# Features of a second group of tokens computed earlier, and its first MLP ahead of its second softmax, in a transformer kernel on one core

## Chip, core and metric

One core of one Trainium2 chip runs the whole program in one launch. The metric is device time in microseconds, from three runs without a profiler; one further execution was recorded by the hardware profiler, and all rows below are from that one.

## What is computed

The input x has 8 sequences of 256 tokens with 256 features. It passes through four attention layers with an MLP each, then a cross attention and a composed MLP. The change touches the first layer alone. What a layer does, cut from the reference:

```python
x = x + self_attention(layer_norm(x, ln1_g[i], ln1_b[i]), Wq[i], Wk[i], Wv[i], Wo[i], bo[i])
h = layer_norm(x, ln2_g[i], ln2_b[i])
x = x + (jax.nn.gelu(h @ W1[i] + b1[i], approximate=False) @ W2[i] + b2[i])
```

Of the eight heads, four are local (softmax over the own and the previous block of 128 tokens, causal), four are linear: with q = softmax(q) over the 32 features of a head and k = elu(k) + 1, in buckets of 64 tokens,

```python
k_cum = jnp.cumsum(bk.sum(axis=-2), axis=-2)
ctx = jnp.cumsum(jnp.einsum('bhund,bhune->bhude', bk, bv), axis=2)
ctx = ctx / (k_cum[..., None] + 1e-06)          # then shifted by one bucket
out = jnp.einsum('bhund,bhude->bhune', bq, ctx)
```

## The kernel before

The 2048 tokens are four groups of 512 (two sequences, four tiles of 128 tokens). A step takes group n through attention while group n - 1 goes through the first matmuls of its MLP and group n - 2 through the second. Every product of 32-bit operands is made of three passes over a high and a low part (`PASSES`), so each matrix that feeds TensorE is split: ScalarE copies the high part, VectorE or GpSimd subtracts it to get the low part. There is no scheduler: each engine has its list of calls, written out by hand, and runs it in order; an engine that waits for a semaphore holds up all that is behind it. The first two steps have their own lists, `first_step` and `second_step`, on TensorE, ScalarE and VectorE; GpSimd uses the general `step`.

The parts, by name, for group n: `pe_qk` (L1427) makes the transposed queries and keys of the local heads; `pe_tok` (L1432) makes, tile by tile, values of all heads and queries and keys of the linear heads (512 columns), which `act_tok` copies into `v8` and `qk`. **Features**: `dve_features` (maximum of each query head, L644, and subtraction, L646), `act_features` (exponentials of keys and queries), `dve_features2` (relu of the keys L651, joining step min-and-add L653 which raises `kf_done`, sum L656, reciprocal, scaling L660 which raises `qn_done`). `pe_qnt` transposes the queries, `pe_ctx` makes the contexts, `dve_ctx` divides them, `pe_lin` applies them, and the result is split by `act_lin_hi` (L1131) and `dve_lin_lo` (L615). **Softmax** of the local heads, for each sequence b of the group: `pe_s` (scores, L1460), `dve_max` (two reductions, L686 and L687), `act_exp` (eight exponentials with sums, L1137), `pe_pt` (transposes, L1502), `act_pt` and `dve_pt` (copies of the transposed probabilities into `pt[b]`), `pe_pv` (products with the values, L1519). `act_pspread` and `pe_pnorm` turn the reciprocals of the sums. `pe_wo` is the output projection, `dve_res1` adds it to x, after GpSimd's `pool_bias`. **Norms**: `ln_moments`, then rstd on GpSimd (`pool_rstd`, L446), then `ln_centred` (L602) and `ln_shifted` (L611); index 0 is the norm ahead of attention (vec_a), 1 that of the MLP (vec_f). **MLP**: `pe_xt` transposes, `pe_h` the eight first products, `act_gelu` a gelu and the high part, `pool_h_lo` the low part on GpSimd (L458). A gelu waits until the low part two before it is done, and `pe_h` of chunk m for the gelu of chunk m - 2. GpSimd's list around the MLP of group 0 is: rstd of its norm, two bias additions, rstd of group 2's first norm, four low parts, a bias addition, four low parts, the low parts of W2.

`pe_busy` (L1564) repeats a matmul of an identity matrix whose result nobody reads.

Much of SBUF is one array, `scratch`, cut into overlapping tiles. `pt[1]` covers columns 1056 to 2592, the same as `qk` (1056 to 2080) and `qexp` (2080 to 2592). The second of the tiles `xh`, columns 7712 to 8736, holds the normed tokens of the MLP's norm.

## Time and profile before

| what | us |
|---|---|
| median of three runs | 977.26 (976.57 to 978.7) |
| the profiled execution | 977.58 |
| its span, first to last instruction | 975.7 |
| TensorE busy | 953.2 (98%); first slice of 24 us: 7 tenths |
| VectorE busy | 670.4 (69%) |
| ScalarE busy | 611.9 (63%) |
| GpSimd busy | 480.7 (49%) |
| chain that ended last | TensorE 88%, VectorE 7%, ScalarE 2% |

Times in the rows are microseconds from the first instruction unless marked ns. PE is TensorE, DVE VectorE, ACT ScalarE, POOL GpSimd. In a timeline a row may hold several instructions of one kind (x6); its length is from the start of the first to the end of the last, ends overlap the next row a little, and the bracket tells how long the engine had been idle and what released it. The busy time of a whole run says little here: the question is when each engine reaches a point in the first 90 us.

### The profile page before, as it was taken

How to read it: one execution, taken by the hardware profiler on the slowest of the kernel's cores; microseconds unless marked ns; L12 is line 12 of the kernel's file. 1: busy time of each engine (PE TensorE's matmuls, PEld its weight loads, DVE VectorE, ACT ScalarE, POOL GpSimd, SP SyncE). 2: the span in 40 equal slices, each digit the busy share in tenths (PEclk: the TensorE clock that was granted, in tenths of full speed). 3: DMA queues.
4: the chain of work that ended last, by engine and by line, in shares of the span. 5: the costliest groups of instructions: out<-in, count | busy, mean ns of one | idle time of the engine just before them, and what ended most of it. 6: DMA issues, size and time to landing. Idle time of an engine off the chain costs nothing.

```text
span 975.7 us, 21317 instructions
## 1 busy us (share of the span) xinstructions
PE 953.2 (98%) x8421; PEld 818.0 (84%) x8421; DVE 670.4 (69%) x1466; ACT 611.9 (63%) x1392; POOL 480.7 (49%) x377
## 2 busy tenths in 40 slices
PE   7989999999999999999999999999999999999998
PEld 4668888888898888888888888888898769998987
DVE  7696777677776867776687768676451777675544
ACT  4777768677786777686776867776726345444220
POOL 3446466357817554774546277653417323006443
PEclk9999999999999999999999999999999999999999
DMA  6111000002010000021000002001047687820001
GB/s 207 55 35 44 7 12 2 17 1 88 1 45 17 2 2 17 11 77 44 18 2 1 18 1 88 1 2 50 2 100 195 141 172 151 175 59 1 22 23 44
DMA packets 71581, 47.55 MB, mean 49 GB/s; under 512 B 44511, under 2 KB 68159, under 8 KB 71487
## 3 DMA queue, kind: packets, MB, share of 16 engines
q1 hardware_dynamic: 71487, 46.27, 18.4%
q8 instruction: 63, 1.03, 0.4%
q14 instruction: 31, 0.25, 0.1%
HBM read 44.16 MB, written 2.10 MB: 47 GB/s over the span
## 4 chain that ended last, share of the span: by engine, by line
PE 88%; DVE 7%; ACT 2%; issue 1%; POOL 1%; DMA 0%; SPq 0%; POOLq 0%; ACTq 0%; DVEq 0%
PE F L1403 21%; PE F L1557 17%; PE A L1403 16%; PE A L1502 4%; PE A L1736 4%; PE A L1729 4%; PE A L1893 3%; PE A L1460 2%; PE A L1519 2%; PE F L1417 2%; PE A L1417 2%; PE F L1396 2%; PE A L1396 1%; PE A L1493 1%; PE A L1476 1%
## 5 line engine op out<-in xcount | busy, mean ns | idle before, releaser
L1403 PE MATMUL F<-xt,w 128*128 128x512 f32 x864 | 217.7, 400 | 1.6 <-DVE xt L615 1.0
L458 POOL TENSOR_TENSOR ht<-scratch,ht 128x512 fp32r<-128x512 f32 x128 | 175.5, 1390 | 41.8 <-ACT ht L1169 40.5
L1403 PEld LDWEIGHTS F<-xt,w 128*128 128x128 f32 x864 | 157.8, 188 | 39.4 <-issue 3.8
L1557 PE MATMUL F<-w,ht 128*128 128x256 f32 x1536 | 189.2, 282 | 0.4 <-POOL ht L458 0.4
L1557 PEld LDWEIGHTS F<-w,ht 128*128 128x128 f32 x1536 | 182.8, 188 | 5.9 <-issue 4.6
L446 POOL TENSOR_TENSOR rstd<-var,minus_half 128x4 f32<-128x4 f32 x32 | 37.6, 1174 | 180.5 <-DVE var L591 179.8
L1166 ACT ACTIVATE scratch<-F,b_now 128x512 f32<-128x512 f32 x128 | 87.4, 683 | 36.8 <-POOL ht L458 18.5
L1403 PE MATMUL A<-wa,xt 128*128 128x512 f32 x372 | 89.8, 397 | 0.0
L453 POOL TENSOR_TENSOR x<-x,vec_f 128x1024 f32<-128x1024 f32 x16 | 38.0, 2376 | 93.2 <-DVE scratch L611 93.2
L1169 ACT ACTIVATE ht<-scratch 128x512 fp32r<-128x512 f32 x128 | 81.0, 632 | 4.1
L1403 PEld LDWEIGHTS A<-wa,xt 128*128 128x128 f32 x372 | 69.0, 188 | 15.9 <-issue 0.2
L1137 ACT ACTIVATE prob<-A,smax 128x128 f32<-128x128 f32 (+1 forms) x128 | 51.8, 431 | 33.7 <-DVE smax L687 33.7
L611 DVE SCALAR_TENSOR_TENSOR scratch<-scratch,rstd,vec_a 128x256 f32<-128x256 f32 x64 | 70.5, 1160 | 0.2
L1105 ACT ACTIVATE scratch<-A 128x256 f32<-128x256 f32 x62 | 23.6, 381 | 64.2 <-PE A L1403 63.8
L615 DVE TENSOR_TENSOR xt<-A,xt 128x512 fp32r<-128x512 f32 x52 | 33.5, 685 | 39.2 <-ACT xt L1090 34.4
L1137 ACT ACTIVATE scratch<-A,smax 128x128 f32<-128x128 f32 (+1 forms) x128 | 51.8, 431 | 12.4 <-DVE smax L687 12.2
L712 DVE TENSOR_TENSOR x<-A,x 128x512 f32<-128x512 f32 x30 | 20.8, 692 | 53.7 <-PE A L1403 53.7
L546 POOL TENSOR_TENSOR trstd<-tvar,minus_half 128x4 f32<-128x4 f32 (+1 forms) x15 | 14.8, 987 | 86.3 <-DVE tvar L815 86.3
L1387 ACT ACTIVATE scratch<-F 128x512 f32<-128x512 f32 x32 | 19.1, 598 | 55.0 <-PE F L1403 52.0
L719 DVE TENSOR_TENSOR x<-F,x 128x256 f32<-128x256 f32 x64 | 26.3, 420 | 35.8 <-PE F L1557 34.7
L583 DVE BATCH_NORM_STATS2 stats<-x 128x6 f32<-128x256 f32 x128 | 44.8, 412 | 2.2 <-DMA x<-in_x_dram 1.7
L1403 PEld LDWEIGHTS A<-wo,at 128*128 128x128 f32 x360 | 43.7, 188 | 1.3
(256 smaller groups left out, 2040.8 us busy)
## 6 DMA issues: line engine op xcount, KB each, us to landing
raw_f<-in_L_attn_W_dram SPq DMA_DIRECT2D x8, 1024.0 KB, 5.7
scratch<-in_L_ffn_fc_B_dram SPq DMA_DIRECT2D x32, 256.0 KB, 4.1
scratch<-in_L_ffn_fc_A_dram SPq DMA_DIRECT2D x32, 256.0 KB, 4.0
raw_f<-in_L_ffn_fc_A_dram SPq DMA_DIRECT2D x32, 64.0 KB, 3.1
scratch<-in_x_dram SPq DMA_DIRECT2D x1, 2048.0 KB, 10.1
raw_f<-in_L_ffn_fc_B_dram SPq DMA_DIRECT2D x32, 64.0 KB, 3.2
x<-in_x_dram SPq DMA_DIRECT2D x3, 512.0 KB, 6.8
out_dram<-x SPq DMA_DIRECT2D x3, 512.0 KB, 2.9
```

Of the source, the lines that this page charges most:

```text
L458: pool.tensor_tensor(ht[:, 1, m, :], hf[:, m % 2, :], ht[:, 0, m, :].bitcast(F32), ALU.subtract).then_inc(h_lo, 1)
L583: last = dve.bn_stats(stats[i][:, t, :], x[:, TILES * p + t, :])
L611: dve.scalar_tensor_tensor(out=xh[i][:, t, :], in0=xh[i][:, t, :], scalar=rstd[i][:, t:t + 1], in1=vec[:, 1, :], op0=ALU.mult, op1=ALU.add ...
L1137: last = act.activation(prob[b][:, h, a:z], A[:, 2 + h, a:z], ACT.Exp, bias=smax[:, b, w, h:h + 1], scale=-1.0, accum_out=psums[:, 2 * b + ...
L1166: act.activation(hf[:, m % 2, :], F[:, m % 2, :], ACT.Gelu, bias=b1_now[:, m:m + 1]).then_inc(gelu_done, 1)
L1169: act.activation(ht[:, 0, m, :], hf[:, m % 2, :], ACT.Copy).then_inc(h_hi, 1)
L1403: last = pe.matmul(out, lhs(a, c), rhs(b, c), start=clear and k == 0, stop=k == len(total) - 1, skip_group_check=not clear)
L1417: last = pe.matmul(out, lhs(a, c), rhs(b, c), start=k == 0, stop=k == len(total) - 1)
L1502: last = pe.transpose(A[:, PT_BANKS[b][r], P * h:P * h + P], prob[b][:, h, P * r:P * r + P], ident[:, :])
L1557: last = pe.matmul(F[:, t % 2, 0:D], ht[:, a, c, P * t:P * t + P], w2[:, b, c, :], start=k == 0, stop=k == len(passes) - 1)
L1729: last = pe.matmul(A[:, 2 * c + s, :], small[r][a][:, P * c:P * c + P], big[r][b][:, 512 * s:512 * s + 512], start=first and k == 0, stop= ...
L1736: last = pe.matmul(A[:, m // 2, D * (m % 2):D * (m % 2) + D], big[r][a][:, P * m:P * m + P], small[r][b], start=first and k == 0 and m % 2 ...
```

## The change

For the second group (n = 1) the linear heads' queries and keys are computed apart from the values, both ahead of the transposes of the first group's probabilities; they go into the memory of the MLP's normed tokens (`xh[1]`), and the features follow at once, in between the first group's work. The values' products follow in two halves. Two new waits keep the memories apart: ScalarE's copy `act_pt(0, 1)` waits for the joining step of the second group (`kf_done` 2), and the centring of the first MLP's norm waits for `qnt_psum` 2 and `ctx_psum` 2. GpSimd's first bias addition waits for `al_lo`. The norm of the first MLP comes ahead of the second group's second maxima, its high part and transposes ahead of the second exponentials, and its first two products ahead of `pe_lin(1)`; ScalarE's `act_lin_hi(1)` stands behind the first gelu. The filler blocks of 9, 7 and 8 matmuls become 5 and 7.

```diff
@@ -83,6 +83,10 @@
         xh = [scratch[:, a:a + 1024].rearrange("p (t d) -> p t d", t=TILES) for a in (6688, 7712)]
+        qk_of = lambda n: xh[1] if n == 1 else qk
+        qexp_of = lambda n: xh[1][:, :, 0:P] if n == 1 else qexp
+        kexp_of = lambda n: qk[:, 0:2, :].rearrange("p t (s d) -> p (t s) d", s=2) if n == 1 else kexp
+        kfeat_of = lambda n: xh[1][:, :, P:2 * P] if n == 1 else kexp
         hf = scratch[:, 8736:9760].rearrange("p (s t) -> p s t", s=2)
@@ -502,6 +506,7 @@
             split_lo(pool, w1_pieces(), w1_hi, w1_ready, 0)
+            pool.wait_ge(al_lo, 1)
             pool_bias(pool, 0, 0, 0)
...
             def step(l, p, attn=True, nxt=True, mlp=True, out=True):
...
@@ -639,26 +644,35 @@
         def dve_features(dve, n):
-            dve.wait_ge(tok_out, 4 * n + 4)
-            q = qk[:, :, 0:P]
+            dve.wait_ge(tok_out, 6 if n == 1 else 4 * n + 4)
+            q, qe = qk_of(n)[:, :, 0:P], qexp_of(n)
             dve.tensor_reduce(qmax[:, :, :], heads(q), AX_X, ALU.max).then_inc(qmax_done, 1)
             dve.wait_ge(qmax_done, n + 1)
...
-        def dve_features2(dve, n):
-            k = qk[:, :, P:2 * P]
+            dve.tensor_tensor(heads(qe), heads(q), over_e(qmax[:, :, :]), ALU.subtract).then_inc(qsub_done, 1)
+        def dve_features_k(dve, n):
+            k = qk_of(n)[:, :, P:2 * P]
             dve.wait_ge(kexp_done, n + 1)
...
-            dve.scalar_tensor_tensor(out=kexp[:, :, :], in0=kexp[:, :, :], scalar=1.0, in1=k,
+            dve.scalar_tensor_tensor(out=kfeat_of(n), in0=kexp_of(n), scalar=1.0, in1=k,
...
+        def dve_features_sum(dve, n):
             dve.wait_ge(qexp_done, n + 1)
...
+            dve.tensor_reduce(qsum[:, :, :], heads(qexp_of(n)), AX_X, ALU.add).then_inc(qsum_done, 1)
...
+        def dve_features_scale(dve, n):
+            qe = qexp_of(n)
...
+            dve.tensor_tensor(heads(qe), heads(qe), over_e(qsum[:, :, :]), ALU.mult).then_inc(qn_done, 1)
+        def dve_features2(dve, n):
+            dve_features_k(dve, n)
+            dve_features_sum(dve, n)
+            dve_features_scale(dve, n)
...
...
@@ -968,27 +985,31 @@
                 dve_prec(dve, 0)
+                dve_features(dve, 1)
                 top_columns()
...
                 dve_pt(dve, 0, 1)
+                dve_features_k(dve, 1)
                 dve_aloc(dve, 0)
+                dve_features_sum(dve, 1)
                 dve_al_lo(dve, 0)
+                dve_max(dve, 1, 0)
+                dve_features_scale(dve, 1)
             def second_step():
-                dve_features(dve, 1)
-                dve_max(dve, 1, 0)
-                dve_features2(dve, 1)
                 dve_res1(dve, 0, 0)
...
                 ln_moments(dve, 1, 0, 0)
-                dve_max(dve, 1, 1)
-                dve_ctx(dve, 1)
+                dve.wait_ge(qnt_psum, 2)
+                dve.wait_ge(ctx_psum, 2)
                 ln_centred(dve, 1, 0, 0, 0)
                 ln_shifted(dve, 1, 0)
+                dve_max(dve, 1, 1)
+                dve_xt_lo(dve, 1, 0)
+                dve_ctx(dve, 1)
                 dve_prec(dve, 1)
-                dve_xt_lo(dve, 1, 0)
                 dve_lin_lo(dve, 1)
@@ -1099,11 +1120,21 @@
         def act_tok(act, n, t):
             act.wait_ge(tok_psum, 4 * n + t + 1)
-            if n == 1 and t == 0:
-                act.wait_ge(pv_psum, 1)
-            ps = tok_bank(n, t)
+            ps = tok_bank(t)
             act.activation(v8[:, t, :, 0:E], ps[:, 0:2 * P].rearrange("p (h e) -> p h e", e=E), ACT.Copy)
             act.activation(qk[:, t, :], ps[:, 2 * P:4 * P], ACT.Copy).then_inc(tok_out, 1)
+        def act_tok_qk(act, s):
+            act.wait_ge(tok_psum, 5 + s)
+            act.activation(qk_of(1)[:, 2 * s:2 * s + 2, :].rearrange("p t d -> p (t d)"), F[:, s, :],
+                           ACT.Copy).then_inc(tok_out, 1)
+        def act_tok_v(act, s):
+            act.wait_ge(tok_psum, 7 + s)
+            act.wait_ge(pv_psum, 1)
+            for t in range(2):
+                last = act.activation(v8[:, 2 * s + t, :, 0:E], F[:, s, D * t:D * t + D].rearrange("p (h e) -> p h e", e=E), ACT.Copy)
+            last.then_inc(tok_out, 1)
         def act_seed(act, n, b):
...
@@ -1298,34 +1339,36 @@
                 act_pspread(act, 0)
+                act_tok_qk(act, 0)
+                weight_hi(w1_pieces()[2:3], w1_hi)
+                act_tok_qk(act, 1)
+                act_features_k(act, 1)
+                act_features_q(act, 1)
                 act_pt(act, 0, 0)
                 act_lin_hi(act, 0)
-                weight_hi(w1_pieces()[2:3], w1_hi)
+                act_pnorm(act, 0)
+                weight_hi(w1_pieces()[3:4], w1_hi)
+                act.wait_ge(kf_done, 2)
                 act_pt(act, 0, 1)
-                weight_hi(w1_pieces()[3:4], w1_hi)
-                act_pnorm(act, 0)
-                act_tok(act, 1, 0)
-                act_tok(act, 1, 1)
+                act_tok_v(act, 0)
                 act_al_hi(act, 0)
-                act_tok(act, 1, 2)
-                act_tok(act, 1, 3)
+                act_tok_v(act, 1)
             def second_step():
-                act_features(act, 1)
                 act_exp(act, 1, 0)
...
                 weight_hi(w2_pieces(), w2_hi)
-                act_exp(act, 1, 1)
-                act_lin_hi(act, 1)
-                act_xt_hi(act, 1, 0)
-                act_pspread(act, 1)
-                act_pt(act, 1, 0)
                 act.wait_ge(b1_ready, 1)
                 act_b1(act, 0)
-                for m in (0, 1):
-                    act_gelu(act, 0, m)
+                act_xt_hi(act, 1, 0)
+                act_exp(act, 1, 1)
+                act_pspread(act, 1)
+                act_gelu(act, 0, 0)
+                act_lin_hi(act, 1)
+                act_pt(act, 1, 0)
+                act_gelu(act, 0, 1)
                 act_pnorm(act, 1)
@@ -1434,16 +1477,32 @@
                 pe.wait_ge(wa_ready, 1)
-            if n == 1 and t >= 2:
-                pe.wait_ge((pnorm_out, aloc_done)[t - 2], 1)
-            product(pe, tok_bank(n, t), lambda a, c: xt[0][:, a, c, P * t:P * t + P],
+            product(pe, tok_bank(t), lambda a, c: xt[0][:, a, c, P * t:P * t + P],
                     lambda b, c: wa[:, b, c, 2 * P:6 * P]).then_inc(tok_psum, 1)
+        def pe_tok_part(pe, s, cols):
+            for t in range(2):
+                last = product(pe, F[:, s, D * t:D * t + D], lambda a, c: xt[0][:, a, c, P * (2 * s + t):P * (2 * s + t) + P],
+                               lambda b, c: wa[:, b, c, cols])
+            last.then_inc(tok_psum, 1)
+        def pe_tok_qk(pe, s):
+            pe.wait_ge((q_out, k_out)[s], 2)
+            pe_tok_part(pe, s, slice(4 * P, 6 * P))
+        def pe_tok_v(pe, s):
+            pe.wait_ge(tok_out, 5 + s)
+            pe_tok_part(pe, s, slice(2 * P, 4 * P))
         def pe_s(pe, n, b):
...
                     pe.wait_ge(tok_out, 2)
+                if n == 1 and b == 0:
+                    pe.wait_ge(pt_out_act, 2)
+                    pe.wait_ge(pt_out_dve, 4)
                 if b == 1:
...
@@ -1627,36 +1688,35 @@
                 top_k()
-                pe_tok(pe, 1, 0)
+                pe_tok_qk(pe, 0)
+                pe_tok_qk(pe, 1)
                 top_columns()
...
                 pe_pt(pe, 0, 1)
-                pe_tok(pe, 1, 1)
+                pe_tok_v(pe, 0)
                 pe_pv(pe, 0)
-                pe_tok(pe, 1, 2)
-                pe_tok(pe, 1, 3)
+                pe_tok_v(pe, 1)
                 pe_s(pe, 1, 0)
                 pe_wo(pe, 0, 0)
-                pe.wait_ge(tok_out, 8)
-                pe_busy(pe, A[:, 1, :], 9)
+                pe_qnt(pe, 1)
             def second_step():
-                pe_qnt(pe, 1)
+                pe.wait_ge(res1, 2)
+                pe_busy(pe, F[:, 0, :], 5)
                 pe_s(pe, 1, 1)
...
                 pe_ctx(pe, 1)
-                pe.wait_ge(res1, 2)
+                pe.wait_ge(ln_rstd[1], 1)
                 pe_busy(pe, F[:, 0, :], 7)
+                pe_xt(pe, 1, 0)
+                for m in range(2):
+                    pe_h(pe, 0, m, 0)
                 pe.wait_ge(ctxn_done, 2)
                 pe_lin(pe, 1)
-                pe_busy(pe, F[:, 0, :], 8)
-                pe_xt(pe, 1, 0)
                 pe_pt(pe, 1, 0)
-                for m in range(2):
-                    pe_h(pe, 0, m, 0)
                 pe_pnorm(pe, 1)
```

Three places in the order; the numbers in front of a row are lines, which differ between the two kernels.

ScalarE in the second step, before, from the last two of the second exponentials (`act_exp(1, 1)`); at<-A is `act_lin_hi`, xt2<-F the high part of the MLP's input, scratch<-precip `act_pspread`, scratch<-F,b1_now a gelu:

```order
L1137 ACTIVATE prob1,psums<-A,smax 128x128
L1137 ACTIVATE prob1,psums<-A,smax 128x256
L1131 ACTIVATE at<-A 128x2x192
L1090 ACTIVATE xt2<-F 128x512 x2
L1151 ACTIVATE scratch<-precip 128x512
L1143 ACTIVATE scratch<-A 128x512
L1160 ACTIVATE b1_now<-b1c 128x8
L1166 ACT_TABLE_LOAD
L1166 ACTIVATE scratch<-F,b1_now 128x512
L1169 ACTIVATE ht<-scratch 128x512
```


The same place after:

```order
L1178 ACTIVATE prob1,psums<-A,smax 128x128
L1178 ACTIVATE prob1,psums<-A,smax 128x256
L1192 ACTIVATE scratch<-precip 128x512
L1207 ACT_TABLE_LOAD
L1207 ACTIVATE scratch<-F,b1_now 128x512
L1210 ACTIVATE ht<-scratch 128x512
L1172 ACTIVATE at<-A 128x2x192
L1184 ACTIVATE scratch<-A 128x512
L1207 ACTIVATE scratch<-F,b1_now 128x512
L1210 ACTIVATE ht<-scratch 128x512
```


The high part of lin stood directly behind the exponentials; it now stands behind pspread, the table load and the first gelu, and the MLP's input ahead of the exponentials.

VectorE in the second step, before, from the first norm's last variance; smax<-A are the maxima, vec_f the MLP's norm, at<-A the low part of lin, scratch<-A copies of transposed probabilities:

```order
L591 TENSOR_SCALAR var2<-mv2 128x4
L686 TENSOR_REDUCE smax<-A 128x4
L687 TENSOR_REDUCE smax<-A 128x4
L667 TENSOR_SCALAR kcum<-A 128x6
L669 RECIPROCAL kcum<-kcum 128x6
L671 TENSOR_TENSOR ctxn<-A,kcum 128x6x32
L602 SCALAR_TENSOR_TENSOR scratch<-x,mv2,vec_f 128x256 x4
L611 SCALAR_TENSOR_TENSOR scratch<-scratch,rstd2,vec_f 128x256 x4
L696 RECIPROCAL precip<-psums 128x16
L615 TENSOR_TENSOR xt2<-F,xt2 128x512 x2
L615 TENSOR_TENSOR at<-A,at 128x2x192
L692 COPY scratch<-A 128x512 x2
```


The same place after:

```order
L596 TENSOR_SCALAR var2<-mv2 128x4
L607 SCALAR_TENSOR_TENSOR scratch<-x,mv2,vec_f 128x256 x4
L616 SCALAR_TENSOR_TENSOR scratch<-scratch,rstd2,vec_f 128x256 x4
L702 TENSOR_REDUCE smax<-A 128x4 x2
L620 TENSOR_TENSOR xt2<-F,xt2 128x512 x2
L681 TENSOR_SCALAR kcum<-A 128x6
L683 RECIPROCAL kcum<-kcum 128x6
L685 TENSOR_TENSOR ctxn<-A,kcum 128x6x32
L713 RECIPROCAL precip<-psums 128x16
L620 TENSOR_TENSOR at<-A,at 128x2x192
L709 COPY scratch<-A 128x512 x2
```


The maxima moved behind the norm; the low part of lin and the copies stand at the end in both, and in both the third group's first norm follows (rows further on).

VectorE in the first step, before, from the reciprocal of the first sums to the local output; wcol is a small copy for later use, scratch<-A the copies of transposed probabilities:

```order
L696 RECIPROCAL precip<-psums 128x16
L782 COPY wcol<-A 64x32 x2
L692 COPY scratch<-A 128x512 x2
L615 TENSOR_TENSOR at<-A,at 128x2x192
L692 COPY scratch<-A 128x512 x2
L701 TENSOR_TENSOR scratch<-A,scratch 128x512
L615 TENSOR_TENSOR at<-scratch,at 128x512
```


The same place after:

```order
L713 RECIPROCAL precip<-psums 128x16
L649 TENSOR_REDUCE qmax<-scratch 128x16
L651 TENSOR_TENSOR scratch<-scratch,qmax 128x4x128
L799 COPY wcol<-A 64x32 x2
L709 COPY scratch<-A 128x512 x2
L620 TENSOR_TENSOR at<-A,at 128x2x192
L709 COPY scratch<-A 128x512 x2
L656 TENSOR_SCALAR scratch<-scratch 128x4x128
L658 SCALAR_TENSOR_TENSOR scratch<-scratch 128x4x128
```


The second group's maximum and subtraction came ahead of the copies, its relu and joining step between them and the local output.

## Rows read from the trace of the kernel before

**Rows 1.** The page, part 2: TensorE's granted clock, tenths, 40 slices of 24.4 us
```profile
PEclk9999999999999999999999999999999999999999
```

**Rows 2.** The stretches: us; each engine's busy us (instructions), clock, DMA share, GB/s
```profile
94.00:500.00 406.00, 404.75 (x3891) 348.41 (x3890) 299.31 (x618) 298.11 (x694) 230.88 (x171) 1.00 0.07 22
```

**Rows 3.** The timeline, TensorE: start, us, engine, line, operation, tiles, count [idle before <- releaser]
```profile
34.70 1.67 PE L1403 MATMUL F<-wa,xt 128*128 128x512 f32 x6
...
41.89 1.51 PE L1519 MATMUL A<-scratch 128*32 128x256 f32 x32
...
46.67 0.94 PE L1460 MATMUL A<-kT,qT 32*128 32x128 f32 x16
...
50.40 2.12 PE L1564 MATMUL A<-ident_bf 128*128 128x512 bf16 x9
53.09 0.63 PE L1469 MATMUL A<-ident,scratch 128*128 128x128 f32 x4 [0.58 <-DVE scratch L660]
...
55.67 1.69 PE L1564 MATMUL F<-ident_bf 128*128 128x512 bf16 x7
58.67 0.87 PE L1493 MATMUL A<-scratch,ctxn 32*32 32x64 f32 x48 [1.31 <-DVE ctxn L671]
59.47 1.90 PE L1564 MATMUL F<-ident_bf 128*128 128x512 bf16 x8
62.03 1.09 PE L1396 MATMUL F<-ident,scratch 128*128 128x128 f32 x8 [0.65 <-DVE scratch L611]
...
76.03 1.04 PE L1396 MATMUL A<-ident,scratch 128*128 128x128 f32 x8
```

**Rows 4.** The timeline, ScalarE, 50 to 92 us
```profile
50.31 0.37 ACT L1137 ACTIVATE scratch<-A,smax 128x128 f32<-128x128 f32 x1 [1.10 <-DVE smax L687]
...
57.96 0.37 ACT L1137 ACTIVATE prob<-A,smax 128x128 f32<-128x128 f32 x1 [1.54 <-DVE smax L687]
...
61.14 0.53 ACT L1131 ACTIVATE at<-A 128x384 fp32r<-128x384 f32 x1
...
63.69 0.63 ACT L1151 ACTIVATE scratch<-precip 128x512 f32<-128x512 f32 x1
...
65.90 1.28 ACT L1166 ACT_TABLE_LOAD   x1 [0.99 <-issue]
67.19 0.69 ACT L1166 ACTIVATE scratch<-F,b_now 128x512 f32<-128x512 f32 x1
...
71.06 0.69 ACT L1166 ACTIVATE scratch<-F,b_now 128x512 f32<-128x512 f32 x1 [0.30 <-POOL ht L458]
...
91.73 1.28 ACT L1121 ACT_TABLE_LOAD   x1
```

**Rows 5.** The timeline, VectorE, 58 to 76 us
```profile
58.53 1.66 DVE L602 SCALAR_TENSOR_TENSOR scratch<-x,mv,vec_f 128x256 f32<-128x256 f32 x4
...
64.56 0.55 DVE L615 TENSOR_TENSOR at<-A,at 128x384 fp32r<-128x384 f32 x1
...
68.06 0.17 DVE L591 TENSOR_SCALAR var<-mv 128x4 f32<-128x4 f32 x1
...
69.73 1.28 DVE L692 COPY scratch<-A 128x512 f32<-128x512 f32 x2
70.93 4.77 DVE L611 SCALAR_TENSOR_TENSOR scratch<-scratch,rstd,vec_a 128x256 f32<-128x256 f32 x4
```

**Rows 6.** The timeline, GpSimd, 38 to 76 us
```profile
38.31 5.03 POOL L401 TENSOR_TENSOR w<-raw_f,w 128x512 fp32r<-128x512 f32 x4
...
68.31 1.19 POOL L446 TENSOR_TENSOR rstd<-var,minus_half 128x4 f32<-128x4 f32 x1 [1.53 <-DVE var L591]
69.48 5.93 POOL L458 TENSOR_TENSOR ht<-scratch,ht 128x512 fp32r<-128x512 f32 x4
```

**Rows 7.** Two lines of VectorE, all runs of each: min/median/max ns, first and last start
```profile
L615 DVE TENSOR_TENSOR at<-scratch,at x16: 971/1300/1358, 45.3 to 701.2; 128x512 fp32r<-128x512 f32 x16
...
L653 DVE SCALAR_TENSOR_TENSOR scratch<-scratch x16: 691/693/1668, 26.5 to 675.9; 128x512 f32<-128x512 f32 x16
```

41 lines of the change are left out of this document (25 added, 16 removed).

## The prediction

> **What bounds the kernel now.** I read the page first, then one row of the stretches, then the timelines of the four engines between 34 and 92 us, since the change touches nothing outside the first two groups of 512 tokens. The page gives TensorE 98% busy, and its granted clock at the upper of the two levels in all 40 slices [rows 1]. Of the stretch from 94 to 500 us it is busy 404.75 of 406 us [rows 2]: behind the second group there is no slack in which a delay could be made up, and none that would swallow a gain. So what counts is one number, by how much TensorE reaches the third group's work earlier or later.
>
> In the changed stretch TensorE's timeline has three blocks of filler matmuls (line 1564, results never read), 2.12, 1.69 and 1.90 us, and 0.58, 1.31 and 0.65 us of idle time behind them [rows 3]: 8.25 us between 50.40 and 62.03 without useful work. That is the pool from which this change could draw. From 62.03 on TensorE's rows follow each other without idle time, up to the next transposes at 76.03 [rows 3]. Beside them three chains run close behind: ScalarE's gelus, of which the third already waits 0.30 us for GpSimd's low part [rows 4]; VectorE's first norm of the third group, with a slow last step of 4.77 us that ends at 75.70 [rows 5]; GpSimd, which takes that norm's rstd and only then the low parts, 1.48 us each (5.93 for four) [rows 6]. A gain up to 62 us is kept only if these three come earlier too.
>
> **The change part by part.** I laid the new instruction lists out by hand with the trace's durations, waits as in the code; the same layout of the old lists gives the third gelu at 70.8 where the trace has 71.06 [rows 4], and the third group's transposes at 75.7 where it has 76.03 [rows 3]. So the layout errs by some 0.3 us.
>
> *First group's end.* TensorE now makes the second group's queries and keys together: 24 matmuls of 256 columns, twice the columns of the 1.67 us row [rows 3], 3.0 us instead of 1.6. They end at 37.7. ScalarE copies the second half by 38.4. VectorE had only waited there; now its queue has the maximum and the subtraction (0.69 each), the small copy, two copies of transposed probabilities (1.28), a low part (0.55), two more copies (1.28) [rows 5], the relu (0.42) and the joining step (0.69) [rows 7]: 45.0, with 0.6 us for contention, below. ScalarE's copy of the second batch's probabilities has a new wait on that step (it overwrites the same memory), so it ends at 45.6, and the products of probabilities and values start there, not at 41.89 [rows 3]. TensorE, done with the first half of the values' products at 43.4, stands idle some 2.2 us. The second half of the values' products and the scores follow: scores at 48.6, not 46.67 [rows 3], 1.9 us late. Only one other wait is added at the front of a queue here: GpSimd's bias addition now waits for the local output's low part. It takes 2.4 us, the output projection that runs beside it 3.0, so it costs nothing while that product lasts.
>
> *Contention.* The subtraction has two operands in SBUF and now lies beside GpSimd's low parts of W1 (38.31 to 43.34) [rows 6]. A VectorE operation of the same width and kind has a median of 1.30 us where GpSimd works beside it, a minimum of 0.97, and the joining step ranges from 0.69 to 1.67 [rows 7]. I take 0.6 (1.30 less 0.69) once; the ends are 0 and 2.0 (two such steps at 1.67).
>
> *The moved features pay back.* Before, six feature steps stood between the maxima of the scores and the residual; now only the scaling does. First exponentials start at 51.7 (50.31 before [rows 4]) but the residual ends at 53.5, 0.6 us earlier than before, and the norm of the first MLP no longer waits behind the second maxima. Its centring waits instead for the context product, since it writes where the queries lay; that product stands behind the second scores, which wait for the end of the first exponentials (3.3 us, 55.1). So centring starts at 57.2, not 58.53 [rows 5], and TensorE's transposes at 60.6, not 62.03 [rows 3]. The fillers, 12 instead of 24, cover less; behind the last block TensorE idles 1.9 us. Gain at this point: 1.4 us, of the 8.25.
>
> *What that costs.* The second maxima (two reductions, 1.8 us) now follow the whole norm on VectorE, and the exponentials they release start at 62.4, not 57.96 [rows 4], 4.4 us late. Only then come pspread (0.63), the table load (1.28), the first gelu and its copy (0.69 and 0.63), and **only behind these the high part of the global attention, lin_hi**: 65.7 + 0.3 (reciprocal) + 3.1 with their overlap gives 69.1; before it ran at 61.14 [rows 4]. VectorE waits for it at the head of its queue, idle for almost 4 us, and behind this wait stand, in this order, the low part, the copies of the first transposed probabilities, the variance of the third group's norm, centring, and the copies of the second batch's probabilities. The variance, begun at 68.06 before [rows 5], comes at 73.25. GpSimd's rstd stands in front of every low part of the MLP: 1.19, then 1.48 [rows 6], so the first low part ends at 76.1, though its input is there at 69.2. The third gelu goes with it: 76.1, not 71.06 [rows 4]. The product with the second batch's probabilities waits for VectorE's copy until 76.2. The slow last norm step starts at 76.1, not 70.93, and ends at 80.9 (it stays beside GpSimd's low parts, so I keep 4.77 [rows 5]); TensorE's next transposes wait for it, at 81.1 against 76.03 [rows 3]. **That is 5.1 us late**; the following rows keep the distance, 5.2 at the third group.
>
> *The sum.* 1.9 lost before the scores, 3.3 won back up to the transposes (together the gain of 1.4), then 6.6 lost between the second exponentials and the third group: 1.9 - 3.3 + 6.6 = 5.2. Against the profiled execution, 977.58 us, that is 982.8; it lies 0.3 over the median of the three runs, so 982.5 in the median's terms. With contention at its ends 0 and 2.0 the sum is 4.6 to 6.6 (981.9 to 983.9), and with 0.5 either way for the layout 981.4 to 984.4.
>
> *A rule weighed.* ScalarE's gelu table load starts 1.0 us after the last copy, at 65.90; the load at 91.73 starts as the copy before it ends, without a gap [rows 4]. In the new order the gelu's load follows pspread at once. The Trainium skill (ScalarE: Activation LUTs, What ACT_TABLE_LOAD costs) puts a drain of about 1.38 us beside the load's 1.28. The load at 91.73 speaks against a drain of its own; by the page's figure the time would be an estimated 1.4 us more, about 983.9.
>
> **The rivals.**
> *The gain holds.* If VectorE's lin_hi wait were short, the 1.4 us at the transposes would reach the third group: 977.3 - 1.4 = 975.9. This decides itself by whether the third gelu starts before about 71. For it: 8.25 us of filler and idle time stand there to be had. Against it: the order on ScalarE and the single queue of GpSimd, which leave no other way than behind the exponentials.
> *No difference.* The loss of 1.9 us at the first group doesn't come, because the joining step is done before TensorE needs the copies; with it goes the 0.6 of contention; and behind the second group all of the idle time that there is, 1.25 us, is used up by the delay: 5.2 - 1.9 - 0.6 - 1.25 = 1.4, 979.0, or 978.7 in the median's terms. For it: VectorE is idle while the second half is copied, and could be early. Against: eight operations stand in its queue between that copy and the joining step.
> *The clock falls.* With half the filler, TensorE is idle in some ten places of up to 2.2 us between 42 and 81. If its granted clock fell from 2.4 to 1.2 GHz for 5 us of products, these would take 10: about 987. Against: in the whole trace it is never lower, not in the first slice of 24 us either, where the page has TensorE busy 7 tenths [rows 1].
> *Contention is heavier*: both features steps and the scaling slowed: 984 to 985.
>
> **How the numbers follow.** Forecast (late by 4 to 6.8 us) 0.74; heavier contention or the table's drain 0.08; clock 0.03; no difference or a small loss 0.09; gain 0.06. A measurement of this kernel can tell about 0.2%, 2 us. Slower by more: 0.85; within: 0.09; faster: 0.06. Time 982.5; the range 980.0 to 985.5 takes the bounds of contention, the drain and a part of a recovery, and leaves out 2 in 10.
>
> **What would show it.** VectorE idle some 3.8 us before the low part of lin (line 620), released by ScalarE; ScalarE idle near 4 us before the third gelu, released by GpSimd; TensorE idle about 2 us before the product of the first group's probabilities and 2 before the second's; transposes of the first MLP at 60.6, of the third group at 81; second exponentials at 62.4. The forecast is wrong if the first low part of the MLP begins before 71, or if the first group's products of probabilities start before 43.

## The result, and the profile after

The changed kernel takes 982.62 us in the median of six runs (981.1 to 985.17), the kernel before 977.33 us in six (976.57 to 978.7). The ratio on record is 1.0058, with a 95% interval of 1.0047 to 1.0069 (that of the medians is 1.0054): slower by 5.3 us in the medians. The profiled execution took 981.47 us, with a span of 979.5; that is 3.8 us more span than before.

Only one execution of each kernel has a trace, but each run of the changed kernel has its mean granted clock on record (1 is the upper level throughout). By it the six runs fall in two groups: three of 981.1 to 981.5 us at 0.996 or 0.997, the profiled one among them, and three of 983.8 to 985.2 us at 0.992 to 0.994. The median lies in the gap between them; no run is within 1 us of it. One run of the variant e5_own_room, of 1413.81 us at a mean granted clock of 0.615, is left out of what follows.

The timeline of TensorE, kernel after (start, us, line, operation, tiles, count, idle time before it and its releaser; line numbers are those of the changed kernel):

```profile
33.02 0.87 PE L1554 MATMUL A<-scratch,ctxn 32*32 32x64 f32 x48
...
34.23 3.08 PE L1446 MATMUL F<-wa,xt 128*128 128x256 f32 x24
...
45.28 1.51 PE L1580 MATMUL A<-scratch 128*32 128x256 f32 x32 [1.84 <-ACT scratch L1184]
...
48.66 0.94 PE L1519 MATMUL A<-kT,qT 32*128 32x128 f32 x16
...
60.61 1.69 PE L1439 MATMUL F<-ident,scratch 128*128 128x128 f32 x8 [2.03 <-DVE scratch L616]
63.03 2.90 PE L1460 MATMUL F<-xt,w 128*128 128x512 f32 x6 [0.73 <-DVE xt L620]
65.72 2.49 PE L1446 MATMUL F<-xt,w 128*128 128x512 f32 x6
...
76.75 1.51 PE L1580 MATMUL A<-scratch 128*32 128x256 f32 x32 [1.72 <-issue]
78.19 3.06 PE L1446 MATMUL F<-xt,w 128*128 128x512 f32 x12
81.42 1.09 PE L1439 MATMUL A<-ident,scratch 128*128 128x128 f32 x8 [0.17 <-DVE scratch L616]
...
90.84 4.38 PE L1446 MATMUL A<-wa,xt 128*128 128x512 f32 x18
```

Three more rows of TensorE's timeline, kernel before:

```profile
33.49 0.87 PE L1493 MATMUL A<-scratch,ctxn 32*32 32x64 f32 x48
...
71.70 1.51 PE L1519 MATMUL A<-scratch 128*32 128x256 f32 x32
...
85.24 5.79 PE L1403 MATMUL A<-wa,xt 128*128 128x512 f32 x24
```

Read against [rows 3], the rows of 34.23, 45.28 and 48.66 are the first loss: queries and keys in one block, then 1.84 us of idle time before the products of probabilities and values (45.28, not 41.89), then the scores at 48.66, not 46.67. The first MLP's transposes at 60.61 are the gain: they stood at 62.03. The rows from 76.75 on are the second loss: the second batch's product with the values comes at 76.75, not 71.70, and at 81.42 stand the transposes of the third group that were at 76.03. The row of 63.03 holds what I had not forecast: six matmuls of 512 columns take 2.90 us; in the row of 78.19 twelve of them take 3.06.

The timeline of ScalarE, kernel after, against [rows 4]:

```profile
62.83 0.36 ACT L1178 ACTIVATE prob<-A,smax 128x128 f32<-128x128 f32 x1
...
66.48 0.63 ACT L1192 ACTIVATE scratch<-precip 128x512 f32<-128x512 f32 x1 [0.32 <-DVE precip L713]
67.13 1.28 ACT L1207 ACT_TABLE_LOAD   x1
68.42 0.69 ACT L1207 ACTIVATE scratch<-F,b_now 128x512 f32<-128x512 f32 x1
69.68 0.47 ACT L1172 ACTIVATE at<-A 128x384 fp32r<-128x384 f32 x1
...
76.66 0.69 ACT L1207 ACTIVATE scratch<-F,b_now 128x512 f32<-128x512 f32 x1 [3.81 <-POOL ht L462]
```

The high part of lin (line 1172) comes at 69.68, not 61.14, and the third gelu waits 3.81 us for GpSimd and comes at 76.66, not 71.06. The timeline of VectorE, kernel after, against [rows 5]:

```profile
70.18 0.56 DVE L620 TENSOR_TENSOR at<-A,at 128x384 fp32r<-128x384 f32 x1 [3.74 <-ACT at L1172]
...
73.70 0.17 DVE L596 TENSOR_SCALAR var<-mv 128x4 f32<-128x4 f32 x1
...
75.37 1.28 DVE L709 COPY scratch<-A 128x512 f32<-128x512 f32 x2
76.56 4.80 DVE L616 SCALAR_TENSOR_TENSOR scratch<-scratch,rstd,vec_a 128x256 f32<-128x256 f32 x4
```

VectorE stands 3.74 us at the head of its queue for ScalarE's high part; the variance behind it slips from 68.06 to 73.70. GpSimd takes it up, against [rows 6] (timeline of GpSimd, kernel after):

```profile
73.95 1.19 POOL L450 TENSOR_TENSOR rstd<-var,minus_half 128x4 f32<-128x4 f32 x1 [8.63 <-DVE var L596]
75.12 2.69 POOL L462 TENSOR_TENSOR ht<-scratch,ht 128x512 fp32r<-128x512 f32 x2
```

So the chain closes: exponentials late, high part of lin late, VectorE's wait, variance, rstd, low part, third gelu; and on VectorE the slow last step of the norm (4.80 us) at 76.56 in place of 70.93, behind which TensorE's transposes wait. Most of the delay is on TensorE before that step: of the 5.39 us at the transposes 5.05 are there at 76.75. The profile names no releaser for the wait of 1.72 us ahead of that row, but the program has it wait for VectorE's copies, and the copy of 75.37, behind the variance and the centring in VectorE's queue, ends at 76.65.

Against [rows 1], where the granted clock has a 9 in all 40 slices, the page of the kernel after (first fence) has an 8 in the third (49.0 to 73.5 us). The windows of the kernel after (us; busy time of TensorE, its weight loads, VectorE, ScalarE, GpSimd; granted clock, DMA share, GB/s) place it:

```profile
PEclk9989999999999999999999999999999999999999
```

```profile
60.00:62.00 2.00, 1.39 (x8) 1.29 (x8) 2.00 (x4) 0.46 (x1) 1.37 (x1) 0.74 0.00 0
62.00:64.00 2.00, 1.27 (x4) 0.83 (x3) 1.85 (x6) 1.80 (x9) 2.00 (x2) 0.50 0.00 0
...
66.00:68.00 2.00, 2.00 (x6) 1.38 (x5) 0.25 (x1) 1.66 (x4) 0.00 (x0) 0.56 0.00 0
68.00:70.00 2.00, 2.00 (x59) 1.77 (x59) 0.00 (x0) 1.96 (x4) 0.00 (x0) 1.00 0.03 8
```

From about 61 to 68 us the clock is at its lower level, 1.2 instead of 2.4 GHz. Before it fell TensorE had been busy 7.89 us of the ten from 50 to 60, and idle for 2.03 just before 60.61. This one fall goes with a mean of 0.996 over the execution; in the runs at 0.992 to 0.994 the clock was down for longer, but no trace shows where.

**A measure for the runs below.** I call *the stretch* the time from the first group's products with the context (line 1554 after, 1493 before; both ahead of everything that the change touches) to the start of the third group's 24 products of 512 columns. Before: 33.49 to 85.24, 51.75 us. After: 33.02 to 90.84, 57.82 us, so **6.07 us more**. The earlier start, 33.02 for 33.49, is scatter: nothing that the change touches stands ahead of it, and in the traces below it lies between 32.96 and 35.01. Of the 3.8 us of span, then, 6.07 comes from the stretch, less 0.47 from the earlier start, and less 1.8 from behind the stretch (975.7 - 85.24 = 890.46 before, 979.5 - 90.84 = 888.66 after).

### The profile page after: what moved, and what is told of

Its sections match the earlier page's. It is cut to its first block, busy times and chain, and to the rows that moved or that the text cites. A ratio compares the mean times of both kernels' runs of the same rounds, so it can differ in the third digit from the quotient of the medians.

```text
span 979.5 us, 21346 instructions
## 1 busy us (share of the span) xinstructions
PE 954.0 (97%) x8433; PEld 819.9 (84%) x8433; DVE 671.8 (69%) x1466; ACT 612.6 (63%) x1390; POOL 480.5 (49%) x377
## 4 chain that ended last, share of the span: by engine, by line
PE 83%; DVE 10%; ACT 4%; issue 1%; POOL 1%; DMA 0%; SPq 0%; POOLq 0%; DVEq 0%; ACTq 0%
PE F L1446 20%; PE F L1618 15%; PE A L1446 15%; PE A L1796 4%; PE A L1563 4%; PE A L1953 3%; PE A L1789 3%; PE A L1519 2%; PE A L1580 2%; PE A L1460 2%; PE F L1460 2%; DVE smax L702 2%; PE F L1439 1%; ACT prob L1178 1%; PE A L1439 1%
## 5 line engine op out<-in xcount | busy, mean ns | idle before, releaser
L1446 PE MATMUL A<-wa,xt 128*128 128x512 f32 x360 | 86.8, 396 | 0.0
L1446 PEld LDWEIGHTS A<-wa,xt 128*128 128x128 f32 x360 | 66.8, 188 | 15.3
L702 DVE TENSOR_REDUCE smax<-A 128x4 f32<-128x512 f32 x64 | 58.0, 947 | 8.9 <-PE A L1519 8.9
```

What stands on the lines that cost most here:

```text
L702: last = dve.tensor_reduce(smax[:, b, w, :], A[:, 2:6, P * w:P * (2 * w + 1)], AX_X, ALU.min)
L1446: last = pe.matmul(out, lhs(a, c), rhs(b, c), start=clear and k == 0, stop=k == len(total) - 1, skip_group_check=not clear)
```

## Experiments

The theory: two losses in series. The first is the new wait of ScalarE's copy on VectorE's joining step (some 2 us on TensorE), the second the late high part of lin with all that is queued behind it on VectorE. The rivals: the fallen clock is what costs, or the first part costs nothing and the second everything, or some of it is the norm's slow step beside GpSimd. The runs came in two sets, each beside runs of the kernel before on the same chip: e1 to e4 (977.24 us, 23 runs) and e5 to e8 (977.77 us, 25 runs). An expectation in us was worked out from some 977.3, so it is the distance from the set's own kernel before that counts.

**e1_fill: is it the clock?** More filler ahead of the first MLP's transposes:

```diff
                 pe.wait_ge(ln_rstd[1], 1)
-                pe_busy(pe, F[:, 0, :], 7)
+                pe_busy(pe, F[:, 0, :], 16)
                 pe_xt(pe, 1, 0)
```

> The changed kernel with 16 instead of 7 filler matmuls ahead of the first MLP's transposes, where its trace has 2.03 us idle, then a granted clock of 0.50 from about 61 to 68 us. Nine fillers are 2.0 us, so TensorE starts the transposes when it did. Theory A (the order of the instructions: ScalarE's high part of lin behind the first gelu, VectorE and GpSimd in a row behind it): the clock stays up, the products of 2.90 and 2.49 us go back to 1.6 and 1.5, but the third gelu moves only by what the second exponentials were late by the slow transposes, some 1.0 us: about 981.3, and the times of the runs lie closer together than 981.1 to 985.2. Theory B (the loss is the clock's): the time falls to the kernel before, 977.3, or below.

Measured: 982.07 us (981.46 to 984.0), ratio 1.0042 (1.0029 to 1.0056). In the trace the clock stayed up at this place. The window from 60 to 70 us and the timeline of TensorE, kernel e1_fill:

```profile
60.00:70.00 10.00, 8.59 (x94) 6.19 (x92) 5.69 (x13) 6.84 (x21) 4.71 (x2) 1.00 0.01 2
```

```profile
64.47 1.64 PE L1460 MATMUL F<-xt,w 128*128 128x512 f32 x6 [1.32 <-DVE xt L620]
65.95 1.56 PE L1446 MATMUL F<-xt,w 128*128 128x512 f32 x6
...
71.64 1.36 PE L1563 MATMUL A<-ident,prob 128*128 128x128 f32 x8 [1.00 <-ACT scratch L1184]
...
77.69 1.51 PE L1580 MATMUL A<-scratch 128*32 128x256 f32 x32 [1.90 <-issue]
```

The twelve matmuls take 1.64 and 1.56 us, not 2.90 and 2.49, and yet the stretch is only 0.5 us shorter (5.56 us over before): TensorE now waits 1.00 and 1.90 us where it had waited 1.72. What bounds is VectorE's chain, and the slower products had only filled the wait. The single runs say the same with the clock up throughout: four of the five, at 0.999 or 1.0, took 981.5 to 982.3 us, and the fourteen runs of the kernel before at such a clock 976.0 to 977.6. So this fall of the clock is not the main cause, and the first rival falls. (The profiled execution is the fifth, 984.0 us at 0.995; its clock fell at 10 to 20 and at 800 to 820 us.)

**e2_mom: VectorE's wait out of the way.** The third group's moments and centring ahead of the step that waits:

```diff
                 dve_prec(dve, 1)
-                dve_lin_lo(dve, 1)
-                dve_pt(dve, 1, 0)
                 dve.wait_ge(res2, 12)
                 ln_scaled(dve, 0, 2, 2, 0)
+                dve_lin_lo(dve, 1)
+                dve_pt(dve, 1, 0)
                 dve_pt(dve, 1, 1)
```

> The changed kernel with the third group's first norm (moments, variance, centring) moved on VectorE ahead of the low part of lin, into the 3.7 us in which VectorE stands idle. Theory A: the variance is there some 3.5 us earlier, GpSimd's rstd no longer holds up the low parts of the MLP, and TensorE reaches the third group 2.6 us earlier: 980.0. The wait for the copies of the second batch's probabilities stays, so not more. Theory B (clock): nothing moves, 982.6, since the clock falls before this place.

Measured: 981.23 us (978.27 to 982.32), ratio 1.0032 (1.0021 to 1.0043); the stretch is 4.16 us over before, 1.9 less than after. The timeline of VectorE, kernel e2_mom, shows the mechanism taken apart:

```profile
67.67 1.66 DVE L607 SCALAR_TENSOR_TENSOR scratch<-x,mv,vec_a 128x256 f32<-128x256 f32 x4
69.99 0.56 DVE L620 TENSOR_TENSOR at<-A,at 128x384 fp32r<-128x384 f32 x1 [0.65 <-ACT at L1172]
...
73.40 1.66 DVE L616 SCALAR_TENSOR_TENSOR scratch<-scratch,rstd,vec_a 128x256 f32<-128x256 f32 x4
```

The wait of 3.74 is 0.65 us, and the norm's last step takes 1.66 us in place of 4.80: it no longer lies beside GpSimd's low parts, of which the second ends at 73.23 and the third starts at 75.47. Behind that TensorE has no wait left up to the third group. What remains of the loss is in TensorE's own rows (timeline of TensorE, kernel e2_mom):

```profile
62.97 2.90 PE L1460 MATMUL F<-xt,w 128*128 128x512 f32 x6 [1.33 <-DVE xt L620]
65.66 2.76 PE L1446 MATMUL F<-xt,w 128*128 128x512 f32 x6
68.35 1.04 PE L1554 MATMUL A<-scratch,ctxn 32*32 32x64 f32 x48
```

The products at the lower clock take 2.46 us more than e1's 1.64 and 1.56, the wait of 1.33 stands ahead of them, and the lin products (0.97 us to the next row's start) now lie in this part and no longer between two fillers. Together 4.8, less the 0.95 us by which the transposes start earlier in the stretch: 3.8 of the 4.16. So the median missed my 980.0 by about half of what the clock costs here: **once the chain of VectorE is cut, the clock, which had been nearly free, is on the path.** The clocks of the single runs bear it out: two of twelve, at 0.999, took 978.3 and 978.5 us, two at 0.996 took 979.5, and eight at 0.992 to 0.994 took 981.1 to 982.3. With the clock up in both, then, the reordering is worth more than was forecast: 978.3 to 978.5 stand against e1's 981.5 to 982.3.

**e3_linhi: the high part of lin first.**

```diff
                 act_exp(act, 1, 1)
+                act_lin_hi(act, 1)
                 act_pspread(act, 1)
                 act_gelu(act, 0, 0)
-                act_lin_hi(act, 1)
                 act_pt(act, 1, 0)
```

> The changed kernel with ScalarE's high part of lin directly behind the second exponentials, ahead of pspread, table load and first gelu (its old place). It then waits for TensorE's lin product, which stands behind the first two MLP products. Theory A: 2.0 us earlier at the third group: 980.6. Theory B (clock): 982.6 or, as ScalarE now waits for products at half clock, later.

Measured: 982.83 us (982.21 to 984.41), ratio 1.0056 (1.0042 to 1.0069); the stretch is 6.31 over before. My expectation of 980.6 fell. In the window of 60 to 70 us the clock is 0.66, as it is in the kernel after. The timeline of TensorE, kernel e3_linhi, says why the expectation fell:

```profile
66.24 2.76 PE L1446 MATMUL F<-xt,w 128*128 128x512 f32 x6
68.93 0.93 PE L1554 MATMUL A<-scratch,ctxn 32*32 32x64 f32 x48
...
74.14 1.09 PE L1563 MATMUL A<-ident,prob 128*128 128x128 f32 x8 [1.95 <-ACT scratch L1184]
```

TensorE makes lin only behind the MLP's products, at 68.93, and these ran at half rate; ScalarE, with the high part now in front, waits for it (timeline of ScalarE, kernel e3_linhi), and pspread, table load and gelu with it:

```profile
69.94 0.49 ACT L1172 ACTIVATE at<-A 128x384 fp32r<-128x384 f32 x1 [3.76 <-PE A L1554]
```

ScalarE now waits 3.76 us, and VectorE behind it waits as long as ever: 4.00 us in the trace of e3, for 3.74. What the new order takes off the front of ScalarE's queue comes back as a wait for lin.

**e7_linhi_fill: both edits** (e1's filler and e3's order), made to tell whether e3 had failed by its idea or by the clock.

> Lin_hi directly behind the second exponentials and the 16 fillers ahead of the first MLP's transposes, in the changed kernel. Moving lin_hi alone brought nothing (982.8) where the clock was at 0.50 during the two MLP products ahead of lin. Theory D (the clock took what the move gives, since ScalarE now waits for lin behind the slow products): with the clock held, 2.0 us less than the changed kernel at the third group, 980.6. Theory E (the move itself is worth nothing): 982.1, as with the fillers alone.

Measured: 980.6 us (979.75 to 981.33), ratio 1.0028 (1.0017 to 1.0039), as expected if the clock was the reason: 2.8 us over its own kernel before, where 3.3 had been expected. The timeline of ScalarE, kernel e7_linhi_fill:

```profile
68.88 0.49 ACT L1172 ACTIVATE at<-A 128x384 fp32r<-128x384 f32 x1 [1.28 <-PE A L1554]
```

ScalarE's wait falls from 3.76 to 1.28 us, VectorE's from 4.00 to 1.52. Against the ratio of 1.0058 of the changed kernel e1 and e3, with 1.0042 and 1.0056, are at most a little better; both edits together give 1.0028, 2.5 to 3 us less. Each cause hides the other. In this profile the clock fell elsewhere, 0.83 in the window from 40 to 50 us, from the 1.84 us wait of the first part on, and two rows of products there take 1.6 us longer; its stretch is 5.34 us over before, and its time, 981.33, is the longest of the seven. The two runs at 0.999 took 979.8 and 980.0 us, some 2 less than e1's at such a clock.

**e4_old_second: the first part of the change alone.** The order from the second exponentials on as in the kernel before, on all three engines (TensorE's part of it here; the fillers are 5, 7 and 8):

```diff
                 pe_ctx(pe, 1)
-                pe.wait_ge(ln_rstd[1], 1)
                 pe_busy(pe, F[:, 0, :], 7)
-                pe_xt(pe, 1, 0)
-                for m in range(2):
-                    pe_h(pe, 0, m, 0)
                 pe.wait_ge(ctxn_done, 2)
                 pe_lin(pe, 1)
+                pe_busy(pe, F[:, 0, :], 8)
+                pe_xt(pe, 1, 0)
                 pe_pt(pe, 1, 0)
+                for m in range(2):
+                    pe_h(pe, 0, m, 0)
                 pe_pnorm(pe, 1)
```

> The first part of the change alone: second group's queries, keys and features early as in the changed kernel, but the second step in the old order on TensorE, ScalarE and VectorE (second maxima and exponentials ahead of the norm, lin ahead of the MLP), with fillers 5, 7 and 8. Theory A: the second part of the change costs most; the first costs the wait of the first group's probabilities for the joining step less what the features no longer take: 1.4 us over the kernel before, 978.7. If the first part costs nothing: 977.3; if it is the larger cost: 981 or more. The clock stays up in each.

Measured: 976.97 us (975.97 to 978.42), ratio 0.9996 (0.9987 to 1.0004). The stretch is 0.63 over before, where my layout had 1.4, and the time is not to be told from the kernel before. TensorE's wait of 1.84 us is there (timeline of TensorE, kernel e4_old_second),

```profile
46.35 1.51 PE L1580 MATMUL A<-scratch 128*32 128x256 f32 x32 [1.84 <-ACT scratch L1184]
```

and the scores come 2.46 us late in the stretch, but 1.9 of that is won back up to the first MLP's transposes, where the kernel before had filler and idle time; the last 0.6 us doesn't show in the median.

**e8_second_alone: the second part alone**, built on the kernel before: its second exponentials behind the norm, on all three engines (TensorE's part):

```diff
                 pe.wait_ge(res1, 2)
+                pe.wait_ge(ln_rstd[1], 1)
                 pe_busy(pe, F[:, 0, :], 7)
-                pe.wait_ge(ctxn_done, 2)
-                pe_lin(pe, 1)
-                pe_busy(pe, F[:, 0, :], 8)
                 pe_xt(pe, 1, 0)
-                pe_pt(pe, 1, 0)
                 for m in range(2):
                     pe_h(pe, 0, m, 0)
+                pe.wait_ge(ctxn_done, 2)
+                pe_lin(pe, 1)
+                pe_pt(pe, 1, 0)
                 pe_pnorm(pe, 1)
```

> The second part of the change alone, on the kernel before: first step, memory and features as before, the second step in the changed order on TensorE, ScalarE and VectorE. Theory A: by the layout the third group starts 4.3 us later than before: 981.5, with the fillers gone perhaps a lower clock in the MLP's first products and 0.5 us more. If the two parts need each other (the loss comes only from both), 977 to 978.

Measured: 982.94 us (981.39 to 985.55), ratio 1.0059 (1.0044 to 1.0073), the whole loss, 5.2 us where the layout had 4.3 and perhaps 0.5 for the clock. The stretch is 4.91 over before; with e4's 0.63 that makes 5.54 of the 6.07. The clock fell here too, behind a wait of 1.86 us: 0.65 in the window of 58 to 60 us and 0.50 in that of 60 to 62, in which lie the seven fillers and the transposes; the products after them ran at the upper level. The timeline of ScalarE, kernel e8_second_alone, has the rows of the kernel after again:

```profile
69.09 0.47 ACT L1131 ACTIVATE at<-A 128x384 fp32r<-128x384 f32 x1
...
76.08 0.69 ACT L1166 ACTIVATE scratch<-F,b_now 128x512 f32<-128x512 f32 x1 [3.81 <-POOL ht L458]
```

**e5_own_room: the two new waits taken away.** The second group's queries and their exponentials move to memory in which nothing is still read, so the copy of probabilities needs no wait, nor does the centring (the places of the keys and their exponentials change too):

```diff
-        qk_of = lambda n: xh[1] if n == 1 else qk
-        qexp_of = lambda n: xh[1][:, :, 0:P] if n == 1 else qexp
+        qk_of = lambda n: xh[0] if n == 1 else qk
+        qexp_of = lambda n: xh[0][:, :, 0:P] if n == 1 else qexp
...
                 ln_moments(dve, 1, 0, 0)
-                dve.wait_ge(qnt_psum, 2)
-                dve.wait_ge(ctx_psum, 2)
                 ln_centred(dve, 1, 0, 0, 0)
...
-                act.wait_ge(kf_done, 2)
                 act_pt(act, 0, 1)
```

> The changed kernel with the second group's queries, keys and features in xh[0], which is free until the third group's norm, and their exponentials in xh[1]: the wait of the copy of transposed probabilities for the joining step and the wait of the MLP's norm for the context product fall away, all else as in the changed kernel. Theory A (order, with the memory waits as its first part): 3.8 us less than the changed kernel at the third group, by the same layout, so about 979, 1.7 over the kernel before; the second part's chain over lin_hi stays. Theory C (the memory waits are hidden by other work): 982.6.

Measured: 978.23 us (eleven runs, 977.23 to 980.17), ratio 1.0007 (0.9997 to 1.0017), not to be told from the kernel before, where 1.7 us more had been expected. The stretch is 2.92 us over before, 3.15 less than that of the kernel after. The timeline of TensorE, kernel e5_own_room:

```profile
43.44 1.51 PE L1577 MATMUL A<-scratch 128*32 128x256 f32 x32
...
57.00 1.09 PE L1436 MATMUL F<-ident,scratch 128*128 128x128 f32 x8 [0.24 <-DVE scratch L616]
...
72.65 2.42 PE L1577 MATMUL A<-scratch 128*32 128x256 f32 x32 [1.90 <-issue]
75.00 3.74 PE L1443 MATMUL F<-xt,w 128*128 128x512 f32 x12
```

The first wait is gone, the transposes start at 57.00, not 60.61; then the second loss comes as before, with its wait of 1.90 us on TensorE and 3.74 on VectorE. Reckoned from the start of the stretch (33.11 here) the scores come 1.91 us sooner than in the kernel after and the transposes 3.70: the wait of the copy is worth 1.9, that of the centring the other 1.8. This time the clock fell behind TensorE's wait (2.42 us for a product of 1.51, 3.74 for 3.06); without that the third group would be an estimated 1.3 us sooner, since VectorE's slow step had ended at 77.23 and the transposes start at 78.58.

**e6_room_old_second: e5's memory and e4's order**, the version that these runs pointed to.

> As the run before, but with the second step in the old order (second maxima and exponentials ahead of the norm, lin and its split ahead of the MLP), fillers 5, 7 and 8. Theory A: the early features now pay, the first part of the change comes without its price: 1.5 us less than the kernel before, 975.7. If the early features are worth nothing, 977.2.

Measured: 975.77 us (973.91 to 978.16), ratio 0.998 (0.997 to 0.9991): 2.0 us faster than its kernel before, where 1.5 had been expected. The stretch is 1.28 us shorter than before's (the layout gave 1.5), and 1.91 shorter than e4's: the wait of the copy again. Against e5 the old order is worth 2.5 us in the medians. So the early queries and keys are worth having, if the copy of probabilities doesn't write where their features are read, and if the second exponentials stay ahead of the norm.

## Why the prediction was right, and where it was not

982.5 us was forecast, 982.62 measured. The chain was as predicted, and the sizes came near; but that the total agrees to 0.1 us is luck. In the profiled executions the forecast was 5.2 us, and 3.9 was measured: the stretch was 0.87 longer than forecast, 1.8 came back behind it, and 0.47 is the earlier start. The median then lies 1.15 us over the profiled execution, halfway to three runs with a lower mean clock.

In terms of the stretch (start to scores, scores to transposes, transposes to third group):

| part | forecast | measured |
|---|---|---|
| lost before the scores | 1.9 | 2.46 |
| won back up to the transposes | 3.3 | 3.41 |
| lost up to the third group | 6.6 | 7.02 |
| together | 5.2 | 6.07 |

*First group's end.* Forecast: the product waits 2.2 us and starts at 45.6, scores at 48.6. Measured 1.84, 45.28 and 48.66. That looks closer than it is: the stretch had begun 0.47 early, so the scores are 2.46 late in it, not 1.9. e5 shows that the wait is due to the shared memory.

*Contention.* I took 0.6 us, once, on the subtraction. The timeline of VectorE, kernel after:

```profile
38.70 0.98 DVE L651 TENSOR_TENSOR scratch<-scratch,qmax 128x512 f32<-128x512 f32 x1
...
42.91 0.95 DVE L656 TENSOR_SCALAR scratch<-scratch 128x512 f32<-128x512 f32 x1
43.90 0.69 DVE L658 SCALAR_TENSOR_TENSOR scratch<-scratch 128x512 f32<-128x512 f32 x1
```

It was 0.29 on the subtraction (0.98 less 0.69) and 0.53 on the relu (0.95 less 0.42), which I had left at its price; the joining step was not slowed. The sum of 0.8 is inside the bounds of 0 and 2.0; its place was only half right.

*The gain at the transposes.* Forecast 60.6 with 1.9 us idle before; measured 60.61 and 2.03. Not 1.4 us though but 0.95 in the stretch (27.59 us from its start against 28.54), since the stretch began 0.47 us earlier.

*The second loss.* Forecast: VectorE idle 3.8 us, third gelu released by GpSimd after nearly 4, variance at 73.25, slow step at 76.1, transposes at 81.1. Measured: 3.74, 3.81, 73.70, 76.56, 81.42. e8 shows that this part alone makes the loss (4.91 of stretch; the layout of its lists gave 4.3), e2 that it goes through VectorE's queue (a reordering there takes 1.9 us off), and e7 that it goes through ScalarE's high part. e5 and e6 add what I had not seen: with the early features and without the two memory waits the same order costs 2.5 us in the medians, half of e8's 5.2. The slow step of the norm, one of the rivals, was not tested by itself, since in e2 it goes together with the wait; in the trace of after TensorE waits 0.17 us for its end (row of 81.42), so there it adds little to what the copies had cost.

*The term that was mis-sized* is the stretch as a whole: 6.07 for 5.2. Here the step that failed is the clock rival. I had given it 3 in 100, arguing that the trace of before never shows the lower clock, not even in a first slice with TensorE 7 tenths busy; it fell, for about 7 us. My price for it, 5 us, was wrong too, the other way: e1 puts it at 0.5 us in the changed kernel, because VectorE's chain hides the rest. The remaining 0.4 would be contention (0.2) and the layout; no run parts the two. That one trace was clean had said nothing: the profiles of the eight variants have low windows of 10 us at different places (0.83 or 0.84 in 10 to 20 us in e1, e4 and e6, 0.83 in 40 to 50 in e7, 0.93 and 0.90 in 50 to 70 in e8, 0.66 in 60 to 70 in e2 and e3, 0.83 in 70 to 80 in e5, 0.83 in 800 to 810 in e2), on much the same code. Nor was the kernel before free of it: of its 23 runs beside e1 to e4 seven have a mean clock of 0.996 or 0.997, and take 978.0 to 979.5 us; fourteen at 0.999 or 1.0 take 976.0 to 977.6.

*What offset it.* 1.8 us came back behind the stretch, where I had found no slack: TensorE's queue is full there [rows 2], and I took it that a delay would be kept in full. The trace of before has two pauses inside a group of matmuls, put down to nothing that the profile shows (timeline of TensorE, kernel before):

```profile
241.00 0.64 PE L1493 MATMUL A<-scratch,ctxn 32*32 32x64 f32 x30 [1.12 <-issue]
...
597.47 0.63 PE L1493 MATMUL A<-scratch,ctxn 32*32 32x64 f32 x26 [0.28 <-issue]
```

The trace of after has neither; 1.40 of the 1.8 us is here. e8, built on the kernel before, has one of 0.75 us near 245, and 889.75 us behind its stretch. In the other variants the time behind the stretch was 888.7 to 889.4 us, or 890.3 and 890.4 in e1 and e2, whose clock fell near 800. So in these traces the step "the distance is kept" failed by some 1.5 us: both traces of kernels with the old first part have such a pause, none of the eight with the new one. e4 has 0.63 us more stretch and 0.3 us less time, though that is within the noise. What these pauses are, and whether they belong to the code or to single executions, stays open: there is one trace of each kernel, and no run here was made to move them.

*The rule weighed.* The table load starts 0.02 us after pspread ends (67.13; 66.48 and 0.63), and the gelu 0.01 after the load: 1.3 us in all. The drain of 1.38 us that the Trainium skill (ScalarE: Activation LUTs, What ACT_TABLE_LOAD costs) gives beside it isn't in this trace; the same page's 1.28 for the load agrees.

*The rivals.* "The gain holds" needed the third gelu before 71; it came at 76.66. "No difference" rested on the joining step being early; it was not, yet its core was half right: e4 shows that the first part costs next to nothing in the end. Its sum took the 0.6 of contention off twice, since the 1.9 holds it; without that it would have said 979.6, or 979.3 in the median's terms.

## What to carry to other kernels

Before an engine's work is pulled forward, look at what stands *behind* the thing that it displaces on each queue: here the exponentials moved back 4.9 us (62.83 for 57.96), and what hurt was one small operand behind them, for which VectorE waited with the next group's norm in its queue. Undo a wait by the memory that causes it, and try each half of a change alone: early features that are worth 2 us with memory of their own (e6) were hidden in a change that lost 5. And when an edit misses its expectation, see which other cost now lies on the path: here clock and order hid each other, so that e1 and e3 brought nothing clear alone and e7, with both, did. One trace tells one execution's clock: look at the clock of every run before a median is explained.

## What the runs showed of the hardware

The granted clock fell from 2.4 to 1.2 GHz for some 7 us in a kernel in which TensorE is busy 97% of the time, behind a wait of 2.03 us and ten microseconds with 7.89 busy; e2 and e3 have the same wait and the same fall. In the two profiles with nine matmuls of filler more (e1, e7) and in e5, where the wait there is 0.24 us, it stayed up at this place. A wait of this length did not always bring it down: the clock fell behind 1.84 us in e7 and 1.90 in e5, and not behind 1.84 in e4 or 1.90 in e1. What decides it no run here shows. Matmuls of 512 columns took 2.90 us for six at the lower level and 1.64 at the upper.

Four norm steps of 128x256 with two operands in SBUF took 1.66 us in e2, where GpSimd was idle meanwhile, and 4.80 in the kernel after, beside GpSimd's low parts (its rows of 75.12 and 78.09, two each). Four such steps in the same kernel at 58.88, with GpSimd idle, took 1.67.
